# Causal attention on one core: the corner scores of two head pairs in one step instead of two

## The reference

```python
x = x + 0.5 * ffn(layernorm(x))
x = x + attention(layernorm(x))      # has a layernorm of its own as well
x = x + 0.5 * ffn(layernorm(x))
```

```python
sim = einsum('bhid,bhjd->bhij', q, k) * 8.0
attn = softmax(where(tril(ones((n, n))), sim, lowest))
o = einsum('bhij,bhjd->bhid', attn, v)
return o @ w_out
```

## Time and profile before

| | |
|---|---|
| median of 3 executions | 269.72 us |
| profiled execution, its own time | 269.82 us |
| its span in the trace | 268.1 us |
| TensorE, ScalarE, VectorE, GpSimd busy | 96%, 81%, 81%, 30% |
| granted TensorE clock over the span | 0.998 |

### The profile page before, as it was taken

How to read it: one execution, slowest core, us unless ns; L and a number is a source line. 1 busy time by engine, 2 the same in 40 slices (tenths; PEclk the granted TensorE clock), 3 DMA queues, 4 the chain that set the end, 5 groups by cost and what they waited for, 6 DMA issues and landing times.

```text
span 268.1 us, 5428 instructions
## 1 busy us (share of the span) xinstructions
PE 258.2 (96%) x1829; PEld 183.6 (69%) x1829; DVE 216.2 (81%) x590; ACT 217.5 (81%) x344; POOL 80.7 (30%) x175
## 2 busy tenths in 40 slices
PE   7999999999999999979998999999999999999995
PEld 6886878888788786533434433378888887888783
DVE  7999899998898987797378587378889678697784
ACT  2897668859878889999999999987777867859673
POOL 6302104204850482664349545520200000200100
PEclk9999999999999999999999999999999999999999
DMA  5741200001012104101314003300004211210311
GB/s 152 219 123 23 58 1 2 0 1 39 2 34 46 42 2 78 40 1 22 62 39 82 2 4 78 80 1 4 0 8 111 42 39 39 39 34 9 80 39 39
DMA packets 33343, 11.51 MB, mean 43 GB/s; under 512 B 24130, under 2 KB 32548, under 8 KB 33316
## 3 DMA queue, kind: packets, MB, share of 16 engines
q1 hardware_dynamic: 33172, 11.11, 17.7%
q10 hardware_dynamic: 144, 0.07, 0.1%
HBM read 4.88 MB, written 2.62 MB: 28 GB/s over the span
## 4 chain that ended last, share of the span: by engine, by line
PE 73%; DVE 8%; ACT 7%; issue 5%; POOL 4%; DMA 2%; SPq 0%; POOLq 0%; DVEq 0%; ACTq 0%
PE ps L590 10%; PE ps L596 10%; PE ps L608 10%; PE ps L593 10%; PE ps L613 10%; PE ps L611 9%; PE ps L746 5%; ACT probs L937 3%; PE ps L708 2%; PE ps L777 2%; ACT h L924 2%; POOL probs L1533 1%; POOL w_raw L1527 1%; DMA kT<-k_stack 1%; DVE h_lo L1100 1%
## 5 line engine op out<-in xcount | busy, mean ns | idle before, releaser
L924 ACT ACTIVATE h<-ps,cols 128x512 f32<-128x512 f32 x128 | 88.0, 694 | 36.2 <-PE ps L596 32.6
L1100 DVE TENSOR_TENSOR h_lo<-h,h_hi 128x512 fp32r<-128x512 f32 x128 | 88.6, 698 | 19.1 <-ACT h_hi L927 16.7
L937 ACT ACTIVATE probs<-ps 128x1024 f32<-128x1024 f32 (+1 forms) x80 | 65.0, 918 | 1.5 <-PE ps L708 1.4
L590 PE MATMUL ps<-xT_hi,w_hi 128*128 128x512 f32 x128 | 51.5, 402 | 0.0
L608 PE MATMUL ps<-h_hi,w_hi 128*128 128x512 f32 x128 | 50.5, 395 | 0.3 <-ACT yT L949 0.3
L927 ACT ACTIVATE h_hi<-ps,cols 128x512 fp32r<-128x512 f32 x73 | 50.2, 688 | 0.0
L613 PE MATMUL ps<-h_lo,w_hi 128*128 128x512 f32 x128 | 50.2, 392 | 0.0
L596 PE MATMUL ps<-xT_lo,w_hi 128*128 128x512 f32 x128 | 49.9, 390 | 0.0
L593 PE MATMUL ps<-xT_hi,w_lo 128*128 128x512 f32 x128 | 49.9, 390 | 0.0
L611 PE MATMUL ps<-h_hi,w_lo 128*128 128x512 f32 x128 | 49.9, 389 | 0.0
L746 PE MATMUL ps<-probs,v_ones 128*32 128x512 f32 (+4 forms) x384 | 34.2, 458 | 0.9 <-POOL probs L1533 0.6
(11 more groups left out here) (141 smaller groups left out, 273.2 us busy)
## 6 DMA issues: line engine op xcount, KB each, us to landing
w_raw<-in_L_ffn_w SPq DMA_DIRECT2D x8, 256.0 KB, 4.6
turned<-blocks SPq DMA_DIRECT2D x6, 256.0 KB, 2.0
w_raw<-turned SPq DMA_DIRECT2D x24, 64.0 KB, 2.3
w_raw<-v_ones SPq DMA_DIRECT2D x8, 128.0 KB, 2.4
x_sb<-in_L_attn_x SPq DMA_DIRECT2D x3, 256.0 KB, 6.8
out_x<-x_sb SPq DMA_DIRECT2D x3, 256.0 KB, 2.3
w_raw<-o_scaled SPq DMA_DIRECT2D x2, 256.0 KB, 4.3
x_sb<-in_L_attn_x SPq DMA_DIRECT2D x2, 128.0 KB, 2.3
```

The lines of the kernel that those rows point to most:

```text
L590: pe.matmul(bank, w1_hi[:, w], xT_hi[:, cols_g], start=True, stop=False)
L924: first = nc.scalar.activation(h[:, slot, :], ps[:, BANK_H + slot, :], ACT.Gelu, bias=bias)
L937: nc.scalar.activation(probs[:, s % P_SLOTS, :, 0:width], ps[:, bank:bank + 2, 0:width], ACT.Exp, scale=SCALE).then_inc(exp_done, 1)
L1100: dve.tensor_tensor(h_lo[:, slot, :], h[:, slot, :], h_hi[:, slot, :].bitcast(f32), ALU.subtract).then_inc(split_done, 1)
```

## The change

The two corner steps of a unit become one. `issued` lists the steps that are issued, without those of pair 1 at corners: 72 of the 80. `score_set` and `set_reader` go by the place in that list. Both pairs' corner scores go into one set of banks, pair 1 at columns 128 to 255 of each bank, and one exponential reads 2 x 256 columns. Between the eight products of pair 0 and the eight of pair 1 the program waits on a new semaphore, `corner_scores`, which the last product of pair 0 raises. `exp_done` and `scores_done` rise by two at such a step. The order `scores, outputs, scores` at corners is gone: both pairs' scores stand ahead of `outputs(k)`. GpSimd's masks keep their number and order and read the new place.

```diff
+        issued = [s for s, st in enumerate(steps) if not (st["corners"] and st["pair"])]
+        place = {s: r for r, s in enumerate(issued)}
+        def exps_until(s):
+            return s + 2 if steps[s]["corners"] else s + 1
         def score_set(s):
-            return s % 2 if s < 4 else (s - 2) % S_SETS
+            r = place[s]
+            return r % 2 if r < 4 else (r - 2) % S_SETS
         def set_reader(s):
-            return s - 2 if s in (2, 3) else None if s == 4 or s < 2 else s - S_SETS
+            r = place[s]
+            return issued[r - 2] if r in (2, 3) else None if r == 4 or r < 2 else issued[r - S_SETS]
...
             def scores(s):
                 st = steps[s]
                 if set_reader(s) is not None:
-                    pe.wait_ge(exp_done, set_reader(s) + 1)
-                for n, (kt, q0, width, at) in enumerate(st["item"]):
+                    pe.wait_ge(exp_done, exps_until(set_reader(s)))
+                products = [(st["pair"], n, 0) for n in range(len(st["item"]))]
+                if st["corners"]:
+                    products = [(pair, n, P * pair) for pair in range(2) for n in range(GROUP_TILES)]
+                for pair, n, offset in products:
...
                     for hd in range(2):
-                        j = 2 * st["pair"] + hd
+                        j = 2 * pair + hd
+                        if pair == 1 and st["corners"] and n == 0 and hd == 0:
+                            pe.wait_ge(corner_scores, st["unit"] + 1)
...
+                    if st["corners"] and pair == 0 and n == GROUP_TILES - 1:
+                        m.then_inc(corner_scores, 1)
-                m.then_inc(scores_done, 1)
+                m.then_inc(scores_done, 2 if st["corners"] else 1)
...
             for k in range(quad_steps):
-                short = steps[2 * k]["last"] and k < quad_steps - 1
                 if k == PV_LAG - 1:
                     third_products(0)
                 scores_of(2 * k)
-                if short:
-                    outputs(k)
-                scores_of(2 * k + 1)
-                if not short:
-                    outputs(k)
+                if not steps[2 * k]["corners"]:
+                    scores_of(2 * k + 1)
+                outputs(k)
...
-            for s in range(3, len(steps)):
+            for s in issued[3:]:
                 exp_scores(s)
```

More of the change, by code:

```diff
@@ L228, in build @@
         third_mm, third_copied = sem("third_mm"), sem("third_copied")
-        corners_zero = sem("corners_zero")
+        corners_zero, corner_scores = sem("corners_zero"), sem("corner_scores")
         corners_in = [sem(f"corners_in{p}") for p in range(GROUPS)]
@@ L359, in step_width @@
         def step_width(s):
-            return max(at + width for _, _, width, at in steps[s]["item"])
+            width = max(at + width for _, _, width, at in steps[s]["item"])
+            return 2 * width if steps[s]["corners"] else width
         V_CORNERS = TILES // 2 * HEADS * ROW
@@ L699, in scores @@
                 if set_reader(s) is not None:
-                    pe.wait_ge(exp_done, set_reader(s) + 1)
-                for n, (kt, q0, width, at) in enumerate(st["item"]):
+                    pe.wait_ge(exp_done, exps_until(set_reader(s)))
[3 more added lines that the diff above has]
+                for pair, n, offset in products:
+                    kt, q0, width, at = st["item"][n]
                     p = Q_GROUPS * st["b"] + st["qg"]
@@ L705, in scores @@
                     for hd in range(2):
-                        j = 2 * st["pair"] + hd
+                        j = 2 * pair + hd
+                        if pair == 1 and st["corners"] and n == 0 and hd == 0:
+                            pe.wait_ge(corner_scores, st["unit"] + 1)
                         rows = slice(ROW * j, ROW * j + ROW)
-                        m = pe.matmul(ps[first_row:first_row + keys, 2 * score_set(s) + hd, at:at + width],
+                        m = pe.matmul(ps[first_row:first_row + keys, 2 * score_set(s) + hd, offset + at:offset + at + width],
                                       kT[rows, kp, st["quad"], k0:k0 + keys],
                                       qT[rows, p, st["quad"], q0:q0 + width], start=True, stop=True)
-                m.then_inc(scores_done, 1)
+                    if st["corners"] and pair == 0 and n == GROUP_TILES - 1:
+                        m.then_inc(corner_scores, 1)
+                m.then_inc(scores_done, 2 if st["corners"] else 1)
             def pv(k):
@@ L824, in outputs @@
                         for c in range(LAG):
-                            pe.wait_ge(exp_done, len(steps) - 2 + c // 2 + 1)
+                            pe.wait_ge(exp_done, len(steps))
                             up(1, GROUPS, c, 0)
@@ L937, in exp_scores @@
                 nc.scalar.activation(probs[:, s % P_SLOTS, :, 0:width], ps[:, bank:bank + 2, 0:width], ACT.Exp,
-                                     scale=SCALE).then_inc(exp_done, 1)
+                                     scale=SCALE).then_inc(exp_done, 2 if steps[s]["corners"] else 1)
             def evacuate_y(F):
@@ L1523, in _ @@
                     for n, rows in enumerate((slice(0, HALF), slice(HALF, P))):
-                        packed = probs[rows, s % P_SLOTS, :, 0:P]
+                        packed = probs[rows, (s - st["pair"]) % P_SLOTS, :, P * st["pair"]:P * st["pair"] + P]
                         spread = corner_probs()[rows, corner_slot(st["unit"], st["pair"]), :, n, :]
```

## The result

| | before | after |
|---|---|---|
| median in the same session | 269.74 us (8 runs) | 270.68 us (8 runs) |
| ratio, 95% interval | | 1.004 [1.0029, 1.0051] |
| profiled execution / its span | 269.82 / 268.1 us | 270.42 / 268.7 us |

One of the eight executions of the changed kernel took 630.43 us and is left out of the ratio; without it the median is 270.67.

What follows compares the result with a forecast made beforehand. TensorE was taken to bound the time at the corners of units 0, 2 and 6, other waits covering the rest; 0.27 + 0.12 + 0.12 = +0.51 us gave 270.2 us against 269.72, whole range 269.3 to 271.1.

Steps and rivals of the forecast that it cites:

- The self-wait and the three places: TensorE waits on itself inside each merged corner block of 0.48 us; counts at units 0, 2, 6: +0.27, +0.12, +0.12 us.
- The upper end of the wait: Slowest release in the rows, 0.25 us and not 0.05, between the pairs' corner products: 0.20 more three times, 1.11 in all.
- The lower end: Merged block as two blocks of 0.18 us with nothing between: adds 0 at units 2 and 6, 0.15 at unit 0.
- the hidden wait: Rival: TensorE's wait between the pairs hides in the drain paid at changes of shape; +0.15, 269.9 us; chance 0.18.
- ScalarE's saving: Eight fewer corner exponentials, each merged one 0.48 us in place of 0.54: 0.5 us of ScalarE's own time.
- worth nothing: Claim that ScalarE's 0.5 us saved at corners gains no time, as TensorE, the DMA or s76 and s77 come last.
- they are off the chain, and behind them stands the DMA: Claim that shorter waits for a free set after corners, such as 0.49 us at 143.29, gain no time.
- the wait of 143.29: TensorE's wait of 0.49 us for a free set at 143.29 us, which the merge was to take away without gain.
- Units 3, 4 and 5 are covered: Their added 3 x 0.12 = 0.36 us on TensorE vanishes in idle times of 0.49 and 0.19 and the late keys.
- The forecast's sign at the keys: Sign of being right: the keys' DMA lands 0.4 us later than at 147.5 and TensorE waits for it.
- Every corner counts: Rival: units 1, 3, 4, 5 and 7 are not covered; 0.27 + 7 x 0.12 = 1.11 us, 270.8 us; chance 0.15.
- ScalarE is the bound: Rival: corner intervals on ScalarE shrink from 0.72 to 0.48, 8 x 0.24 = 1.9 us faster, 267.8 us; chance 0.14.

Runs made afterwards that it cites:

- its control: The kernel before with the same 64 waiting instructions put into TensorE's program in the first stage, nothing joined: 269.73 us, 0.9999 [0.999, 1.0008].

## Why the prediction was right, and where it was not

The parts, as medians, all against the kernel before of their session or its control:

| part | forecast | measured |
|---|---|---|
| units 0, 2, 6 | +0.51 | +0.68 |
| units 1, 7 | 0 | 269.67 - 269.75 = -0.08, interval holds zero |
| units 3, 4, 5, fetch shifted | 0 | 269.46 - 269.73 = -0.27 |
| the fetch on the keys' issue | not there | 270.68 - 269.99 = +0.69 |
| sum | +0.51 | +1.02, the whole change +0.94 |

The profiled executions, from unit 0's corners to the `pv` behind s77 (63.49 us before), give the same list with less noise: +0.57 for units 0, 2 and 6, -0.09 for 1 and 7, 172.24 - 109.00 - 63.49 = -0.25 for 3 to 5 with the fetch shifted, and +0.47 for the fetch. That is +0.70, and the change has +0.75.

*The self-wait and the three places: right.* Block 0.51 us for 0.48 forecast; in the profiled execution +0.29, +0.15 and +0.15 where 0.27, 0.12 and 0.12 stood. Together that is 0.59, and the trace of the run with those three units alone has 0.57; its median gave 0.68, with an interval of 0.35 to 0.86 that holds the forecast too. In the change, 0.08 of it is gone by unit 2's corners: the scores of s22 and s23 hold TensorE 123.86 - 123.34 = 0.52 us, before 123.78 - 123.19 = 0.59. With 1 and 7 joined they take 0.52 as well, and with 0, 2 and 6 joined 0.59, so this is won by unit 1's join: s23 waits for s20's exponential (before, that ends at 123.40 and s23's products begin at 123.46), and ScalarE comes to it earlier. The forecast had put unit 1 at nothing.

*Bounds.* The upper end of the wait, 0.25 us for a release, was not reached, as pair 1 began 0.05 us behind pair 0's modelled end; the wait put in by hand at unit 0 cost 0.16 of idle time, so 0.05 is not a constant. The lower end, the hidden wait, fell with the blocks of 0.51 and with the kernel that has the wait at unit 0 alone: 0.39 us more of block were 0.44 us more of time.

*ScalarE's saving: 0.48 us from start to start of a corner exponential as forecast* (143.23 to 143.70 in the trace), *but "worth nothing" failed at unit 5.* The failing step is the sentence on waits for a free set, "they are off the chain, and behind them stands the DMA". That holds for the wait of 143.29 that it named. It does not hold for s53, whose scores come behind the DMA: there the free set was the last thing waited for, and with one set fewer in use 0.18 us were won. The kernel that joined 3 to 5 and kept the fetch away gained 0.27, in the trace 0.25. The rest of it, some 0.08, lies between the keys' landing and the first scores: 0.13 us in its control, 0.05 joined (landing at 147.41, scores at 147.46). Why is not shown.

*"Units 3, 4 and 5 are covered": right for TensorE's own cost, blind for what rides on its place in the program.* The term that is missing from the sum is the instruction fetch, +0.69 by the medians. In the profiled executions it is smaller: counted from unit 0's corners, the `pv` behind s77 comes 0.47 later without the shift (173.23 - 108.99 = 64.24) than with it (172.85 - 109.08 = 63.77). The first issue is 0.54 longer there, and the DMA behind it 0.08 shorter (3.12 against 3.20). Both profiled executions of the change took 270.42 us, 0.26 less than the median; what its slower executions do more is in no trace.

*The total.* 0.51 of the 0.94 stood for the right reason. The rest is +0.69, -0.27 and -0.08 of terms that the forecast lacked and +0.17 by which the run with units 0, 2 and 6 lay above the sum. Without the fetch, the change costs 269.99 - 269.73 = 0.26 us (0.28 in the traces). That the time lies inside the range is luck in part: the room above the forecast's 270.2 was there for a dearer wait and for the other five corners, and what filled it was the fetch. The forecast's sign at the keys missed: they landed 0.72 us later and not 0.4.

*Rivals.* "Every corner counts" gave 270.8, nearest to the time, by a mechanism that is not there: units 1 and 7 cost nothing and 3 to 5 gain. "ScalarE is the bound" fell: its 267.8 is far from every run, and in the kernel with `pv` between the pairs ScalarE has its whole saving and the time stayed. At two places, unit 1's corners and s53, ScalarE does bind, for 0.09 and 0.18 us. The rule of the Trainium skill (TensorEngine Tiling (Array Packing), Restrictions and Gotchas) on row tiles and one PSUM bank was respected in every run, so none shows what happens without the wait. That its price is the overlap is shown: 0.21 us side by side in separate banks, 0.51 in one bank with the wait, 0.60 in separate banks with a wait.

## What to carry to other kernels

Merging two instructions of a busy engine pays only where that engine is the last one waited for; here eight exponentials fewer were worth 0.18 us at one place and 0.09 at another, and the wait that came with them cost 0.57 at three others. Before pricing a merge, look at what its operands must now share: two groups of products that ran side by side in separate banks stood one behind the other once they wrote one bank and a wait kept them apart. Count places in a trace from a mark close by (here unit 0's corners): the parts then added up to within 0.05 us. And when a DMA or its issue changes its length while nothing near it was edited, look for an instruction fetch in the trace's DMA records: padding an engine's program in a covered stage tells in one run whether it is that, and a kernel that seems worse by 0.5 us may turn out better than the one before.

## What the runs showed of the hardware

- TensorE's program comes in fetches of 16 KB that take 0.9 to 1.5 us here. With 64 more instructions in the first stage the fetches at 142.5 us (before) and 143.3 (the change) came at 140.2 both, and the one of 145.0 at 139.8 with units 3 to 5 joined. In the four traces in which it reached into the transposes' packets, these took 3.2 to 3.8 us and not 2.8; one of SyncE's two issues grew in three of them, from 1.25 to 1.79 and 1.72 or from 1.33 to 2.40. In the two in which it began among them the keys' DMA took 4.2 and not 3.2, with more than 1 us of near standstill. A fetch that ended before their first packet, even one that ran into the issue, cost nothing that shows.
- Why joining corners moves the fetch as it does stays open. Counted in TensorE's products, it came at the 981st before, the 991st in the change and the 1025th with 3, 4 and 5 joined, though the program has the same number of instructions; its place is not its boundary alone. The changed kernel and the one with 3, 4 and 5 joined, padded, had it at the 925th, both.
- A wait of 1.35 us for those keys, with units 1, 3, 4, 5 and 7 joined, was followed by a lower clock in the profiled execution (stretch, busy time of PE, PEld, DVE, ACT, POOL, granted clock, DMA share, GB/s):

```profile
148.00:149.00 1.00, 0.32 (x4) 0.10 (x4) 0.00 (x0) 0.00 (x0) 0.85 (x4) 1.00 0.14 28
149.00:150.00 1.00, 1.00 (x12) 0.37 (x12) 0.00 (x0) 0.89 (x1) 0.78 (x3) 0.69 0.00 0
```

  0.69 is a mean between the two levels, 2.4 GHz (1.00) and 1.2 GHz; in the two microseconds after it the granted clock is 0.50, the lower level. From the first scores behind the keys to unit 6's corners this execution took 160.90 - 148.69 = 12.21 us. With units 3, 4 and 5 joined TensorE idled 1.33 us at the same place, kept 1.00 and took 159.63 - 148.54 = 11.09 us over the same work:

```profile
149.00:150.00 1.00, 1.00 (x17) 0.42 (x14) 0.00 (x0) 1.00 (x2) 0.78 (x3) 1.00 0.09 25
```

  So a fetch at a bad place was followed by a loss of 1.1 us more in one execution and by none in the other, which fits the wide spread of these two kernels (269.67 to 271.8 and 269.38 to 271.84 us).
